# Attention scores from 48 rows of float32r parts, two heads side by side in the array, in a fused post-norm layer

## The reference

```python
q = jnp.dot(x, Wq).reshape(b, t, H, HD).transpose(0, 2, 1, 3)
kv = jnp.dot(x, Wkv).reshape(b, t, G, 2, HD).transpose(2, 3, 0, 1, 4)
...
scores = jnp.einsum('bhqd,bhkd->bhqk', q, k)
scores = jnp.where(causal[None, None], -jnp.inf, scores)
weights = jax.nn.softmax(scores * (1.0 / HD ** 0.5), axis=-1)
ctx = jnp.einsum('bhqk,bhkd->bhqd', weights, v)
x = _layernorm(x + jnp.dot(ctx.transpose(0, 2, 1, 3).reshape(b, t, d), Wo) + bo)
base = jnp.einsum('bsd,od->bso', x, W) + bias
x = _layernorm(x + base + lora_out)
```

## Time and profile before

| what | us |
|---|---|
| the three runs | 404.04, 406.26, 406.14 |
| their median | 406.14 |
| span of the profiled execution, first to last instruction | 405.6 |

### The profile page before, as it was taken

One profiled execution on the slowest core, in us unless ns is written; L12 is line 12 of the kernel. 1 busy time (PEld: TensorE's weight loads), 2 busy tenths in 40 slices (PEclk: granted clock), 3 DMA queues, 4 the chain that ended last, 5 costly groups with the idle time before them and its releaser, 6 DMA issues.

```text
span 405.6 us, 6517 instructions
## 1 busy us (share of the span) xinstructions
PE 347.4 (86%) x2148; PEld 170.0 (42%) x2148; DVE 289.6 (71%) x1036; ACT 210.4 (52%) x398; POOL 108.2 (27%) x193
## 2 busy tenths in 40 slices
PE   4880588929999789999999998999999999998992
PEld 2760355415454333344342333434433333426871
DVE  3340298645888889999769986699897987205985
ACT  4360033615655657677556774567665575692110
POOL 1270023313344345352203022020130202220431
PEclk9996599968999989999999998999999999999997
DMA  7636863240411011110100101000000000000002
GB/s 237 182 103 155 251 153 106 57 135 2 118 42 37 8 39 43 42 40 0 42 0 29 39 3 40 2 27 3 0 3 26 4 1 2 2 27 2 0 27 78
DMA packets 20523, 21.33 MB, mean 53 GB/s; under 512 B 5834, under 2 KB 16010, under 8 KB 20490
## 3 DMA queue, kind: packets, MB, share of 16 engines
q1 hardware_dynamic: 20490, 20.92, 17.9%
HBM read 14.68 MB, written 6.03 MB: 51 GB/s over the span
## 4 chain that ended last, share of the span: by engine, by line
PE 52%; DVE 23%; SPq 7%; DMA 6%; ACT 5%; issue 4%; POOL 2%; POOLq 0%; DVEq 0%; ACTq 0%
PE PS L964 13%; PE PS L1091 12%; PE PS L936 11%; PE PS L1112 9%; SPq L412 6%; DVE MX L720 5%; DVE MX L725 4%; DVE scrap L728 3%; DMA QS<-scr_q 3%; ACT PB L673 2%; DMA QS<-NMR 2%; PE PS L1026 2%; DVE stats L812 2%; PE PS L1034 2%; DVE TC L822 1%
## 5 line engine op out<-in xcount | busy, mean ns | idle before, releaser
L673 ACT ACTIVATE PB<-PS 128x512 f32<-128x512 f32 (+1 forms) x304 | 157.0, 582 | 90.7 <-PE PS L1112 89.8
L936 PE MATMUL PS<-KS,QS 96*128 96x512 bf16 (+3 forms) x384 | 112.5, 338 | 35.4 <-DMA QS<-scr_q 15.9
L1112 PE MATMUL PS<-QS,KS 99*128 99x512 bf16 (+3 forms) x384 | 121.2, 334 | 1.3 <-ACT VX L596 0.4
L569 POOL TENSOR_SCALAR_AFFINE_SELECT PB<-PB 128x256 f32<-128x256 f32 x128 | 51.8, 410 | 187.6 <-ACT PB L673 187.1
L725 DVE TENSOR_REDUCE MX<-PS 128x1 f32<-128x384 f32 (+2 forms) x160 | 75.6, 473 | 14.9 <-PE PS L936 14.6
L1091 PE MATMUL PS<-PB,VX 128*32 128x512 f32 (+3 forms) x768 | 82.5, 502 | 1.2 <-POOL PB L569 1.2
L720 DVE TENSOR_REDUCE MX<-PS 128x1 f32<-128x512 f32 x128 | 80.8, 682 | 2.6 <-PE PS L936 2.2
L728 DVE CUSTOM_DVE_ANT_0 scrap<-PS,mask 128x128 f32<-128x128 f32 x256 | 66.3, 282 | 16.6 <-PE PS L936 16.6
L936 PEld LDWEIGHTS PS<-KS,QS 96*128 96x128 bf16 x384 | 35.2, 100 | 93.1 <-DVE MX L728 24.4
L1112 PEld LDWEIGHTS PS<-QS,KS 99*128 99x128 bf16 x384 | 36.8, 99 | 40.3 <-ACT PB L673 19.9
L964 PE MATMUL PS<-XT,WQ 128*128 128x512 f32 x144 | 45.0, 454 | 3.6 <-DVE WQ L872 3.1
(11 more groups left out here) (69 smaller groups left out, 264.1 us busy)
## 6 DMA issues: line engine op xcount, KB each, us to landing
scr_q<-parts SPq DMA_DIRECT2D x8, 384.0 KB, 4.1
QS<-scr_q SPq DMA_DIRECT2D x16, 192.0 KB, 3.0
X<-in_L_attn_x_dram SPq DMA_DIRECT2D x8, 256.0 KB, 6.4
QS<-scr_q SPq DMA_DIRECT2D x16, 128.0 KB, 3.0
out_dram<-TC SPq DMA_DIRECT2D x8, 256.0 KB, 2.0
RAW<-in_L_attn_Wq_dram SPq DMA_DIRECT2D x1, 1024.0 KB, 8.2
QS<-scr_q SPq DMA_DIRECT2D x16, 64.0 KB, 3.0
RAW<-in_L_attn_Wo_dram SPq DMA_DIRECT2D x1, 1024.0 KB, 12.5
```

Of the source, the lines that this page charges most:

```text
L569: nc.gpsimd.affine_select(out=blk, in_=blk, compare_op=ALU.is_ge, fill=0.0, base=0, pattern=[[0, 2], [1, P]], channel_multiplier=-1)\
L673: nc.scalar.activation(PB[:, cyc % NP_BUF, heads[0]:heads[-1] + 1, d * P:HT], PS[:, score_bank(e), 0:len(heads) * (HT - d * P)] .rearrange ...
L936: last = nc.tensor.matmul(PS[:, n % MAX_BANKS, k * width:(k + 1) * width], QS[0:ROWS, u % SLOTS, j, qb * P:(qb + 1) * P], KS[0:ROWS, g, k0 ...
L1112: last = nc.tensor.matmul(PS[:, score_bank(e), place * width:(place + 1) * width], KS[0:NROW, u % G, kb * P:(kb + 1) * P], QS[0:NROW, u % ...
```

## The change

- Queries and keys are split into two float32r parts instead of three bfloat16 parts: 3 products by 16 dimensions are 48 rows, 51 with the maxima. Two heads lie in partitions 0 to 50 and 64 to 114, and a pair of matmuls, each in its own half of the array's rows, writes two neighbouring banks.
- A chunk is now a pair of heads in two banks. The other half's keys are read by one reduction over two banks (2 x 512); the own half's by one masked operation per head over its whole width, against a bfloat16 mask of 512 columns. ACT's exp reads two banks at once.
- Chunks and scores share three slots of two banks, in the order in which they are made; PE waits for whatever was in the slot before (`slot_free`).
- The third part goes (ACT's `middle_part`, POOL's `low_part`). Keys are loaded by 6 DMAs of 16 rows each, the first two groups apart and ahead (`ks_first`), queries by 4 DMAs for each unit. Rows of ones come by DMA, maxima move by 2 DMAs for each unit instead of 3.
- `T1` turns a unit's context two cycles after the unit ended, once for all four query blocks, into CTX for all 1024 positions; `T1a` and `T1b` go from the steps and from the tail.
- SBUF is laid out anew: W now lands where the attention bias lay. So W, the low-rank matrices and Wo are loaded only after the second half's keys were issued and after POOL added the bias to all of X (`xr_ready`), which it now does in one go.
- Query slots are 4 instead of 5; `DUE` is leveled with other costs.

```diff
-    ROWS = 6 * HD
+    ROWS = 3 * HD
     NROW = ROWS + NPART
+    PAIR = 2
+    NPAIR = REP // PAIR
+    TILE = P // PAIR
...
-    SLOTS = 5
+    SLOTS = 4
...
+    CHUNKS = [(u, qb, own, i) for u in range(NU) for qb in range(TB)
+              for own in ((0, 1) if half_of(u) else (1,)) for i in range(NPAIR)]
...
+    FILL = dict(zip((0, 3, 4, 7, 8, 11, 12, 15, 16), LATER))
+    for u in range(NU - 1):
+        FILL[FIRST[u + 1] + 2] = ("T1", u, 0)
+    STEP_KINDS = ("T2", "WO", "T3", "FF")
...
+    MADE = [("M", n, n % 2) for n in range(DUE[0])]
+    for c in range(NCYC):
+        for i, lot in enumerate(chunks_of_cycle(c)):
+            for kind, n in [("M", n) for n in lot] + [("S", NPAIR * c + i)]:
+                MADE.append((kind, n, (len(MADE) - DUE[0]) % 3))
+    SLOT = {(kind, n): slot for kind, n, slot in MADE}
+    BEFORE = {}
+    for k, (kind, n, slot) in enumerate(MADE):
+        BEFORE[kind, n] = next(((a, b) for a, b, other in reversed(MADE[:k]) if other == slot), None)
...
             for n in range(PROJ_A):
...
                 if n == 1:
-                    load_keys(0)
+                    load_keys(0, slice(0, 2), ks_first)
                     load_queries(0)
                     load_queries(1)
+                    load_keys(0, slice(2, G), ks_in[0])
...
+            load_keys(1, slice(0, G), ks_in[1])
+            sp.wait_ge(xr_ready, NT)
+            sp.dma_start(w_raw, w.rearrange("(c p) n -> p c n", p=P)).then_inc(w_in, 16)
+            sp.dma_start(a_raw, lora_a.rearrange("n r d -> (n r) d")).then_inc(ab_in, 16)
...
             def chunk_max(n):
...
+                if own:
+                    width = (qb + 1) * P
+                    if n >= 2:
+                        dve.wait_ge(max_read, n - 1)
+                    for t in range(PAIR):
+                        last = nc.vector.tensor_tensor_reduce(
+                            out=scrap[:, PAIR * (n % 2) + t, 0:width], in0=banks[:, t, 0:width], in1=mask[:, HT - width:HT], scale=1.0,
+                            scalar=LOWEST, op0=ALU.add, op1=ALU.max, accum_out=part[:, PAIR * i + t, 1:2])
+                else:
+                    last = nc.vector.tensor_reduce(part[:, PAIR * i:PAIR * (i + 1), 0:1], banks, AX, ALU.max)
...
+            def slot_free(kind, n):
+
+                if BEFORE[kind, n]:
+                    other, k = BEFORE[kind, n]
+                    pe.wait_ge(max_read if other == "M" else probs, k + 1)
+
             def chunk_scores(n):
...
+                slot_free("M", n)
+                for t in range(PAIR):
+                    rows = slice(t * TILE, t * TILE + ROWS)
+                    last = nc.tensor.matmul(bank_pair("M", n)[:, t, 0:width],
+                                            QS[rows, u % SLOTS, i, qb * P:(qb + 1) * P],
+                                            KS[rows, g, k0:k0 + width], start=True, stop=True)
...
             for cyc, (u, kb) in enumerate(CYCLES):
                 if kb == 0:
-                    pe.wait_ge(nm_in, 16 * NPART * (u + 1))
-                for j, lot in enumerate(chunks_of_cycle(cyc)):
+                    pe.wait_ge(nm_in, 16 * PAIR * (u + 1))
+                for i, lot in enumerate(chunks_of_cycle(cyc)):
                     for n in lot:
                         chunk_scores(n)
-                    head_scores(cyc, j)
-                    if j % 2:
-                        filler(cyc, j // 2)
+                    pair_scores(cyc, i)
+                    filler(cyc, i)
```

More of the change, by code:

```diff
@@ L118, in score_width @@
         return HT - max(0, kb - TB * half_of(u)) * P
-    SCORE_BANKS = [0]
-    for c in range(NCYC):
-        SCORE_BANKS.append(SCORE_BANKS[-1] + len(heads_in_banks(score_width(c))))
     PLAN_A = [(("xT", 0, c), 0) for c in range(NC)]
@@ L910, in _ @@
                     second_norm(b)
-                elif kind == "T1":
-                    for k in range(2):
-                        normalise_context(b, k, tail_bank(kind, i) + k)
                 else:
@@ L1064, in _ @@
             pe.wait_ge(consts, 6)
+            pe.wait_ge(ones_in, 16 * PAIR)
             def filler(cyc, part):
@@ L1135, in _ @@
             pe.wait_ge(max_read, len(CHUNKS))
-            pe.wait_ge(probs, SCORE_BANKS[NCYC])
+            pe.wait_ge(probs, NPAIR * NCYC)
             pe.wait_ge(*freed(MISC_ORDER[-1]))
+            for part in range(3):
+                pe_step("T1", NU - 1, MISC, part)
             for kind, i in TAIL:
@@ L1140, in _ @@
                 bank = tail_bank(kind, i)
-                if kind == "T1":
-                    for k, half in enumerate(("T1a", "T1b")):
-                        if i >= 2:
-                            pe.wait_ge(ctx_ready, 2 * (b - 2) + k + 1)
-                        for part in range(3):
-                            pe_step(half, b, bank + k, part)
-                    continue
                 if kind in ("T2", "T3") and i >= 2:
```

376 lines of the change are left out of this document (156 added, 220 removed).

## The result

The changed kernel takes 491.8 us (median of 4 runs, 489.1 to 493.9) against 405.1 for the kernel before (4 runs, 403.3 to 406.3): a ratio of 1.212, interval 1.207 to 1.217. It is 21% slower, far outside the range. The profiled execution has a span of 491.2, which is 85.6 more than before.

The account below looks back on a forecast made before the run. PE was taken as the bound of units 8 to 14 with DVE close behind, the start and end bound otherwise. Terms -13, 0, -5, -3.5 and +8 sum to -13.5: 392.1 us span, 392.6 median, range 375 to 419.

Parts of the forecast that it names:

- Rival B: Whole kernel: locks on shared slots and a lower clock after PE's stands take the gain, 402 to 405 us; chance 0.18.
- Bound by PE, DVE close behind: Units 8 to 14 before the change: PE needs 22.5 of 25.1 us a unit, DVE 20.5.
- Second half, -13: Units 8 to 14: paired matmuls at one stream's cost bring a unit from 25.1 to 23.3 us, 13 in all.
- First half, 0: Cycles 4 to 31: PE's work falls but the new leveling clumps chunks, 87.1 against 87.35 us; bounds -6 and +6.
- The walk through the clumped cycles: First half: cycle-by-cycle estimate with up to 8 chunk pairs in one cycle and none in neighbours, giving 87.1 us.
- Start, -5: Up to unit 1: earlier first chunk, then PE stands for POOL's first triangle; unit 1 at 84 instead of 88.65 us.
- rival D: Start: small pieces of the low-rank matrix queue behind the keys, unit 1 at 95, kernel 404 us; chance 0.06.
- Last unit and tail, -3.5: Kernel's end: ten exps instead of 20 save 0.5 to 1 us, one context turn left in the tail saves 2.5.
- Tile changes, +8: Around fillers: borders between half rows and whole array cost 2 x 0.1 x 40 filler cycles; bounds 0 and 16 us.
- Rival A: Chunk and score pairs: weight loads don't hide or streams run in turn, a pair 0.46, kernel 419 us; chance 0.18.
- break-even: Chunk and score pairs: at a price of 0.35 us a pair the gain of 13.5 us is gone.
- the loop: Cycles with two chunk pairs: second scores wait for the first chunk's slot, 2.84 or 2.5 us a round.

Follow-up runs that it names:

- the kernel with all rows: Changed kernel, each matmul of a pair over all rows from 0 to 111 or 114, one after the other: 470.7 us.
- late weights: Changed kernel, W, low-rank matrices, their weights and Wo loaded in cycle 1, POOL's scaling of the low-rank matrix in cycle 6: 478.8 us.
- 29 with pairs: Changed kernel, DVE reading only 64 columns of each bank of a chunk: 463.1 us.
- 33 with all rows: Changed kernel with each matmul over both heads' rows, DVE also reading only 64 columns of each bank: 437.9 us, against 470.7 without the short reads.
- 48 and 51 rows in the same order: Changed kernel, both heads of a pair made from the same rows 0 to 50, so its matmuls run one after the other: 653.5 us.
- rows of zeros: Changed kernel, matmuls reading 61 or 64 rows of their half, the added ones zeros: 489.2 us; the same with every pair issued twice: 490.1 us.
- doubled pairs: Changed kernel, every pair of matmuls of chunks and scores issued twice into the same banks: 494.9 us.
- late DMAs spread: Kernel before with the early start, cycle 3's DMAs spread over cycles 2 to 5 and 9 to 14, POOL's scaling in cycle 7: 384.6 us, ratio 0.944.

## Why the prediction was wrong

Two steps failed. The first is the large one: the sum had no term for what matmuls over half of the rows do to the granted clock. Rival B had one, but put it at 8 us and tied it to stands of PE. If PE alone set the time, the lower level cost 66 us in units 1 to 14 (118.9 x 0.29 + 208.7 x 0.155) against 6 before. The second is the -13 of the second half: the price of a pair left out the 0.10 that the first pair of each row costs, and the borders between tile shapes were counted too low.

- **Bound by PE, DVE close behind:** right. But I read "PE is the bound" as "less time in use is less time". What PE's matmuls do in that time had a price too.
- **Second half, -13:** failed. A unit took 29.8 and not 23.3, and most of that is the clock. The pair, put at 0.22 to 0.23, was right inside a row of pairs (0.233) and 0.10 short for the first of each row. 111 pairs of units 8 to 14 are such first ones, 16 a unit: 1.6 us, nearly the whole gain of 1.8. So the change gains nothing even where the clock is full: unit 8, the one unit at full clock throughout, took 25.3, and in the kernel before 23.7 at full clock. DVE's 1024 elements, put at a step of 1.13, step by 1.14; the 1.22 of the record has the tail in it.
- **First half, 0 (bounds -6 and +6):** failed by +35. The walk through the clumped cycles can't be judged, since the clock of 0.72 lies over it; 88 us at full clock against 83 leave +5 for it, within its bounds.
- **Start, -5:** the mechanism was right, its size and place were not. First chunk forecast at 33, measured 30.86; a stand on POOL's first triangle in cycle 1, forecast as 57 to 75, came up to 85.6, 11.3 long. The second half's keys were issued at 60.3, behind parts of Q at 59.9 that I had put at about 51; so the low-rank matrix could be issued only at 65.5, and it took 14.6 instead of 10.2. Unit 1 at 99.4, outside 79 to 89; rival D (95) was the closest.
- **Last unit and tail, -3.5:** +6.3 and +1.3. ACT was not the bound of the last unit any more; PE was 86% busy there at a clock of 0.92.
- **Tile changes, +8:** the price was right and the number was low. At a border between pairs and matmuls of the whole array the step grows by about 0.10 (from a filler of 512 columns to a pair 0.326, 26 times, where it was 0.23 before), and the 48 rows in the kernel before show the same without pairs or float32r. I had counted 80 borders; 154 are recorded in units 1 to 14, so about 15 us at full clock instead of 8, still inside the bounds. At the values nothing is added: 1.00 for full width in both kernels, and 0.33 against 0.31 from scores into them. The drain of which the Trainium skill speaks ("TensorEngine Tiling (Array Packing)", "Key Properties") agrees with the 0.10 at the borders, for which the page has no price.
- **Rival A** (a pair at 0.46) fell, in that two tiles do run together, as "TensorE: Matmul & The Clock Gate", section "Part 3: Packing small matmuls — row/col tiling" of the Trainium skill has it. Its other sentence, that a load overlaps a running matmul only where the row group differs, is not borne out: 17 of 18 pairs behind a pair in the same rows step by 0.23, and the kernel with all rows steps by 0.235. The break-even that I had set at 0.35 for every pair was reached by the first of each row only (0.34).
- **Rival B** (locks and clock) named the clock, at about a seventh of its size (+8). Its sign, PEclk at 8 tenths or less between 100 and 350, is the one that came. But I let the clock fall only where PE stands. The runs showed that it falls where PE is 97% busy, if the rows at work are half as many (the kernel before with half its rows: +78). DVE's hold on the slots is worth 29 to 33; the walk had the loop in it (23.3 a unit where PE alone needed 18.4), so this can't be set against B's +2 for the locks.

**Where the 85.6 went:** the start 13 (late weights); DVE's hold on the three slots about 30 (29 with pairs, 33 with all rows); the rest, some 40, is lower clock, borders and first pairs, which these runs don't separate to the microsecond, since each makes the others dearer. That fewer rows can lower the clock as far as this is shown in the kernel before. That the changed kernel has its clock because of its rows is shown by giving each matmul more of them: all rows 0.944 against 0.607 with 48 and 51 rows in the same order, and rows of zeros 0.838 against 0.804 and 0.947 against 0.903. The doubled pairs (0.903) add no rows but time, and that raised the clock too.

Left open: why the clock is lower in the first half (0.72) than in the second (0.84) of the changed kernel, and whether the 0.10 of a first pair is a load that doesn't hide or something else.

## What to carry to other kernels

Before packing matmuls into fewer rows of the array, price the clock as well as the time in use: in this kernel, halving the rows at work cost 78 us with the number of matmuls and their columns unchanged, and two tiles side by side gave back only a part. Count the borders between tile shapes and the rows of pairs between them as well, at 0.10 us each here. Try the cheap half first: the same matmuls with fewer rows, the result be what it may, and read the granted clock. And take a change apart before judging it: the order of the start, which was a side effect here, was worth 4.2% to the kernel before once it stood alone, and 5.6% with its late DMAs spread.

## What the runs showed of the hardware

- The granted clock went with the rows that matmuls use. At PE 97% busy it was 0.81 with 48 rows, where 96 and 99 rows at 96% had 0.99. Rows holding zeros counted (0.804 to 0.838, 0.903 to 0.947).
- Issuing every pair twice cost nothing in units 1 to 7 (110.7 against 118.9 us), since the clock rose from 0.71 to 0.94.
- With PE in use for about the same time per pair, two row tiles of 51 rows side by side (each pair issued twice) had a clock of 0.90, and two matmuls one after the other in the same 51 rows 0.61.
- A step between a matmul over half of the rows and one over the whole array took 0.09 to 0.15 us more than one without a change of shape (0.33 against 0.23 behind 512 columns). With all rows in use it took nothing more (0.23).
- The first of a row of two-tile float32r pairs stepped by 0.34 at 512 columns (33 times), the later ones by 0.23 (17 of 18).
- Three DMAs whose source is repeated 3, 2 and 1 times held SP for 11.45 us; the same bytes as twelve DMAs of one copy each took 6.6.
- A reduction over two banks, 1024 elements, stepped by 1.14 us, where two over 512 step by 1.20: one instruction less saved 0.05.
